# Weights prepared between the first graph's steps, on one core of a Trainium2 chip

## What is computed

```python
h = relu(layernorm(x));  x = x + L0(h, adj)     # 8-head attention over adj, then a sigmoid
h = relu(layernorm(x));  x = x + L1(h, adj)     # one symmetric attention, a gate
h = relu(layernorm(x));  x = x + L2(h, adj)     # 5 rounds of message passing with a GRU cell
h = relu(layernorm(x));  x = x + L3(h, adj)     # 1x1 and 17-tap convolutions, exp(-distance)
                                                # weights, a GRU cell
```

## Time and profile before

| | us |
|---|---|
| median of 3 runs | 2305.72 |
| lowest and highest run | 2302.09, 2308.01 |
| profiled execution, its own time | 2308.35 |
| span of the profiled execution | 2306.5 |

### The profile page before, as it was taken

The page is one execution under the profiler, slowest core; times in us unless marked ns, Lnnn a source line. Parts: engine busy times, 40 slices in busy tenths (PEclk is TensorE's granted clock), DMA queues, the critical chain, the costliest instruction groups (busy, mean ns, idle before and its releaser), DMA issues. The chain is left out here.

```text
span 2306.5 us, 36323 instructions
## 1 busy us (share of the span) xinstructions
PE 2122.3 (92%) x12626; PEld 1787.2 (77%) x12626; DVE 1666.9 (72%) x4784; ACT 1506.2 (65%) x2964; POOL 794.1 (34%) x888
## 2 busy tenths in 40 slices
PE   3889999998999999899998999999899999999966
PEld 3769788796978878787786978879697887868744
DVE  3668686877868787786867868687786868778643
ACT  1949485684948668395775939577494866849532
POOL 0333334342343434334243333333333343423311
PEclk7989999999999999999999999999999999999988
DMA  3010001010010101001010000101001010100100
GB/s 117 28 38 13 30 24 37 29 38 28 1 37 28 38 28 37 24 6 38 28 38 28 20 26 21 38 29 38 28 1 42 24 37 28 38 10 1 38 5 5
DMA packets 46791, 65.73 MB, mean 28 GB/s; under 512 B 3728, under 2 KB 21392, under 8 KB 46352
## 3 DMA queue, kind: packets, MB, share of 16 engines
q1 hardware_dynamic: 46608, 63.41, 8.4%
HBM read 59.21 MB, written 4.19 MB: 27 GB/s over the span
## 5 line engine op out<-in xcount | busy, mean ns | idle before, releaser
L573 PE MATMUL banks<-F,PT 128*128 128x128 f32 x4096 | 545.1, 276 | 3.5 <-ACT PT L834 2.8
L573 PEld LDWEIGHTS banks<-F,PT 128*128 128x128 f32 x4096 | 505.4, 192 | 27.6 <-issue 11.7
L1114 DVE COPY PT<-banks 128x512 f32<-128x512 f32 x256 | 176.1, 688 | 156.6 <-PE banks L567 156.1
L869 ACT ACTIVATE F<-banks,dcols 128x512 f32<-128x512 f32 x288 | 193.3, 682 | 27.1 <-PE banks L465 23.3
L431 POOL TENSOR_TENSOR HS<-HT,HS 128x512 fp32r<-128x512 f32 x64 | 83.3, 1301 | 366.7 <-ACT HS L898 366.7
L834 ACT ACTIVATE PT<-banks 128x512 f32<-128x512 f32 x256 | 150.4, 587 | 75.5 <-PE banks L567 75.2
L368 POOL TENSOR_TENSOR rstd<-var,mhalf 128x4 f32<-128x4 f32 x64 | 79.7, 1245 | 324.3 <-DVE var L1017 324.3
L398 POOL TENSOR_SCALAR tiles<-tiles,rden 128x512 f32<-128x512 f32 x192 | 131.9, 696 | 172.4 <-DVE rden L1104 172.2
L398 POOL TENSOR_SCALAR U<-U,rden 128x512 f32<-128x512 f32 x192 | 137.6, 729 | 134.7 <-DVE rden L1104 134.7
L461 PE MATMUL banks<-HS,WH 128*128 128x512 f32 (+1 forms) x368 | 165.2, 449 | 1.6 <-ACT HS L797 1.4
L398 POOL TENSOR_SCALAR adjT<-adjT,rden 128x512 f32<-128x512 f32 x128 | 93.8, 736 | 202.2 <-DVE rden L1104 202.2
(11 more groups left out here) (208 smaller groups left out, 5488.9 us busy)
## 6 DMA issues: line engine op xcount, KB each, us to landing
adjN<-in_adj_dram SPq DMA_DIRECT2D x32, 1024.0 KB, 5.2
adjT<-in_adjt_dram SPq DMA_DIRECT2D x16, 1024.0 KB, 5.4
xin<-in_x_dram SPq DMA_DIRECT2D x18, 256.0 KB, 2.8
out_dram<-X SPq DMA_DIRECT2D x16, 256.0 KB, 2.3
F<-in_c2w_dram SPq DMA_DIRECT2D x1, 1088.0 KB, 9.0
F<-in_wraw_dram SPq DMA_DIRECT2D x1, 1076.0 KB, 9.8
PT<-in_fcw_dram SPq DMA_DIRECT2D x1, 512.0 KB, 3.8
PT<-in_fpw_dram SPq DMA_DIRECT2D x1, 512.0 KB, 5.2
```

What stands on the lines that cost most here:

```text
L573: last = pe.matmul(B[s][:, 3, part(j)], PT[s][:, k, part(j)], G[s][:, k, h * DIM:(h + 1) * DIM], start=(h == 0 and j == 0 and k == 0), sto ...
L869: act.activation(F[s][:, tile, :], B[s][:, bank, :], func, bias=dcol(bias), scale=0.5)\
L1114: dve.tensor_copy(PT[s][:, j, :], pt_bank(s, j)).then_inc(S["pt_dve"], 1)
```

## The change

The setup block is taken apart into a strand called weights, which only graph 0 has, on TensorE (5 steps), ScalarE (5) and VectorE (9), and every weight array has its own semaphore. Loads are issued in the order cols, x of graph 0, the fc pair, adjacency of graph 0, raw weights, prew, c2, adjacency of graph 1, and, after waits for asym_banked and c2_low, x of graph 1. The staging places change: raw stays in F[1], prew goes to PT[1], c2 to adjT[1] and xin[1]. M and WI2 are no longer copied out of PSUM: ScalarE and VectorE split them from the banks.

```diff
+            load(cols[:, :], cols_d, cols_loaded)
+            inputs(0)
+            load(PT[0][:, 0:2, :].rearrange("p t n -> p (t n)"), fcw, fc_loaded)
+            load(PT[1][:, 0:2, :].rearrange("p t n -> p (t n)"), fpw, fc_loaded)
+            masks(0)
+            load(raw, wraw[:, 0:WALL - WRAW], raw_loaded)
...
+            masks(1)
+            sp.wait_ge(asym_banked, 1)
+            sp.wait_ge(c2_low, 1)
+            inputs(1)
...
-            pe.wait_ge(w_loaded, 7 * 16)
...
-            pe.wait_ge(w_split, 4)
+            def weights(g):
+                yield
+                if g > 0:
+                    return
...
+                pe.wait_ge(fc_loaded, 2 * 16)
+                pe.wait_ge(setup_dve, 2)
+                for h in range(HEADS):
+                    pe.matmul(B[1][:, 2, 2 * h:2 * h + 2], fcT[:, part(h)], cols[:, CI["qw"]:CI["qw"] + 2])
+                pe.matmul(B[1][:, 3, 0:HEADS], dcol("qkw").broadcast_to([P, P]), cols[:, 0:HEADS]).then_inc(vq_banked, 1)
+                yield
+                for h in range(HEADS):
+                    last = pe.matmul(B[1][:, h // 4, (h % 4) * DIM:(h % 4 + 1) * DIM], fcT[:, part(h)], fp[:, part(h)])
+                last.then_inc(m_banked, 1)
+                yield
+                pe.wait_ge(vq_ready, 1)
...
+                    .then_inc(m_banked, 1)
+                yield
+                pe.wait_ge(asym_ready, 1)
...
+                yield
+                pe.wait_ge(pre_loaded, 16)
+                pe.wait_ge(raw_ready, 1)
+                pe.wait_ge(m_low, 2)
...
+                last.then_inc(wi_banked, 1)
...
-            act.activation(WH[:, 0:WFIRST], stage[0], ACT.Copy).then_inc(w_split, 1)
-            act.activation(WH[:, WFIRST:WALL], stage[1][:, 0:WALL - WFIRST], ACT.Copy).then_inc(w_split, 1)
-            act.activation(VQH[:, :], VQ[:, :], ACT.Copy).then_inc(setup_act, 1)
-            act.wait_ge(setup_dve, 7)
+                act.wait_ge(vq_ready, 1)
+                act.activation(VQH[:, :], VQ[:, :], ACT.Copy).then_inc(vq_high, 1)
+                yield
+                act.wait_ge(m_banked, 1)
+                act.activation(WH[:, WFIRST:WRAW].rearrange("p (t n) -> p t n", t=2), B[1][:, 0:2, :], ACT.Copy).then_inc(m_high, 1)
+                yield
+                act.wait_ge(raw_ready, 1)
+                act.activation(WH[:, WRAW:WALL], raw, ACT.Copy).then_inc(raw_high, 1)
+                yield
+                act.wait_ge(wi_banked, 1)
...
+                act.activation(tiled(WH), adjT[1][:, :, :], ACT.Copy)
+                act.activation(WH[:, C2A:C2B], xin[1][:, 2, :], ACT.Copy).then_inc(c2_high, 1)
```

More of the change, by code:

```diff
@@ new lines @@
+    ("SP", "transfers"): (3515.678, 3562.397, 3562.397, 3575.622, 3634.067, 3711.988),
+    ("Pool", "inputs"): (3230.966, 3241.946, 3349.882),
+    ("Pool", "normalized"): (3291.779, 3291.779, 3291.779, 3291.779, 3291.779, 3291.779, 3293.808, 3298.303,
[31 rows of a table added]
+    ("Activation", "values"): (3320.761, 3330.097, 3334.275, 3344.175, 3345.848),
+    ("Activation", "weights"): (3235.044, 3313.964, 3344.300, 3360.600, 3389.275),
+    ("Activation", "softmax"): (3337.481, 3337.481, 3338.408, 3339.981, 3342.015, 3344.700, 3344.990, 3348.414,
[6 rows of a table added]
@@ L469, in W @@
                 return WH[:, a:a + n], WLO[:, a:a + n]
-            pe.wait_ge(w_loaded, 7 * 16)
-            fcT = PT[0][:, 0:2, :].rearrange("p t n -> p (t n)")
-            fp = PT[1][:, 0:2, :].rearrange("p t n -> p (t n)")
-            for h in range(HEADS):
-                pe.matmul(B[0][:, h // 4, (h % 4) * DIM:(h % 4 + 1) * DIM], fcT[:, part(h)], fp[:, part(h)])
-            for h in range(HEADS):
-                pe.matmul(B[0][:, 2, 2 * h:2 * h + 2], fcT[:, part(h)], cols[:, CI["qw"]:CI["qw"] + 2])
@@ L480, in _ @@
-            pe.wait_ge(setup_dve, 2)
-            pe.matmul(B[0][:, 3, 0:HEADS], dcol("qkw").broadcast_to([P, P]), cols[:, 0:HEADS])
-            for h in range(HEADS):
-                pe.matmul(B[1][:, 0, 0:DIM], cols[:, h:h + 1].broadcast_to([P, P]), fp[:, part(h)], start=(h == 0), stop=False)
-            pe.wait_ge(ident_ready, 2)
-            pe.matmul(B[1][:, 0, 0:DIM], col("fpb").broadcast_to([P, P]), ident[:, :], start=False, stop=True)
-            pre = PT[0][:, 2:4, :].rearrange("p t n -> p (t n)")
@@ L778, in taps, with weights @@
                 last.then_inc(S["c2_banked"], 1)
-            in_order("PE", values, keys, heads, layer1, layer2, layer3, taps)
+            in_order("PE", weights, values, keys, heads, layer1, layer2, layer3, taps)
         @block.scalar
         def _(act):
-            act.wait_ge(w_loaded, 7 * 16)
-            act.wait_ge(setup_dve, 3)
-            act.activation(WH[:, 0:WFIRST], stage[0], ACT.Copy).then_inc(w_split, 1)
-            act.activation(WH[:, WFIRST:WALL], stage[1][:, 0:WALL - WFIRST], ACT.Copy).then_inc(w_split, 1)
-            act.activation(VQH[:, :], VQ[:, :], ACT.Copy).then_inc(setup_act, 1)
-            act.wait_ge(setup_dve, 7)
+            def weights(g):
+                yield
+                if g > 0:
+                    return
+                act.wait_ge(vq_ready, 1)
[6 more added lines that the diff above has]
+                act.activation(WH[:, WRAW:WALL], raw, ACT.Copy).then_inc(raw_high, 1)
+                yield
+                act.wait_ge(wi_banked, 1)
+                for w, bank in zip(wi_parts(WH), wi_banks):
+                    last = act.activation(w, bank, ACT.Copy)
+                last.then_inc(wi_high, 1)
+                yield
+                act.wait_ge(c2_loaded, 2 * 16)
+                act.activation(tiled(WH), adjT[1][:, :, :], ACT.Copy)
+                act.activation(WH[:, C2A:C2B], xin[1][:, 2, :], ACT.Copy).then_inc(c2_high, 1)
             def h_high(g, turn):
@@ L944, in layer3 @@
                 cand_act(g, cell, "bih3n")
-            in_order("Activation", values, softmax, tile_copies, layer1, layer2, layer3)
+            in_order("Activation", weights, values, softmax, tile_copies, layer1, layer2, layer3)
         @block.vector
@@ L1318, in layer3 @@
                 add_residual(g, 3)
-            in_order("DVE", values, softmax, denominators, tile_copies, layer1, layer2, layer3)
+            in_order("DVE", weights, values, softmax, denominators, tile_copies, layer1, layer2, layer3)
 def kernel(**inputs):
```

192 lines of the change are left out of this document (123 added, 69 removed), and 102 rows, old and new, of the table TURN.

## The result

| | before | after |
|---|---|---|
| median, us | 2304.93 | 2184.37 |
| lowest and highest run, us | 2302.09 to 2308.01 | 2182.48 to 2186.99 |
| span of the profiled execution, us | 2306.5 | 2185.1 |

The ratio is 0.9477, with a 95% interval of 0.9461 to 0.9494.

The account below looks back on a forecast made before the run. TensorE, busy 92% of the span, was taken as the bound. From 2308.35 us, 25 for the front and 52.5 for graphs 1 to 15 (3.5 each) left 2230.9 profiled, median 2228 us; range 2208 to 2287.

Parts of the forecast that it names:

- The front: Stretch up to graph 0's tanh, 123.8 us before; the new setup was to save net 25 us, bounds 18 to 31.
- third weights step: TensorE's nine setup products ahead of graph 0's qk step, 18 matmul records, taken at 4.3 us.
- qk step: TensorE step after the third weights step in graph 0, taken at 2.8 us, giving QK at 23.3 us.
- the splits: ScalarE's raw, WI2 and c2 splits inside graph 0's softmax, 6248 columns, taken at full price, 5.5 us.
- Hole 1: TensorE's wait for layer 1's hN, slowed beside GpSimd's weights3 products; its removal was to save 3.9 us a graph.
- hole 2: TensorE's idle place between layer 3 of one graph and another's first steps; gain taken at zero, bounds -1 and +0.9.
- The dense stretch: Steps between the two holes, where TensorE does not idle; swaps there were to lose 0.4 us a graph, 2.5 at most.
- Theory C: Theory at the start of the experiments, not in the prediction: the order between the holes carries the rest of the gain.
- The first pitch: Spacing from graph 0's tanh to the next, 125.0 us before; forecast to gain 3.5 us like every later graph.
- Only the front: Rival: the order is neutral, 0 +/- 1.5 us a graph, only the setup gains; 2281 us, chance 0.32.
- weak front: Rival: the serial setup chain and softmax splits give back more, net 12 us at the front; 2241 us, chance 0.08.
- slower one: Rival: ScalarE runs dry between the holes, opening a third hole, 3.9 us a graph; 2339 us, chance 0.08.

Follow-up runs that it names:

- before_w3_wait: Kernel before, with GpSimd's four weights3 products waiting until the next graph's hN of layer 1 are done; 2240.9 us (0.9713).
- both waits: Kernel before, GpSimd's weights3 products waiting for the next graph's layer 1 hN, its second layer 1 product for layer 3's xc low part; 2228.9 us (0.9647).
- after_hole1_back_w3_wait: Changed kernel with hole 1's old order put back, and GpSimd's weights3 products waiting for the next graph's layer 1 hN; 2208.5 us (0.9574).
- after_hole2_back2: Changed kernel with the old order around hole 2 put back on TensorE, VectorE and ScalarE; 2195.3 us (0.9523).
- after_hole1_back: Changed kernel with the old order at hole 1 put back on TensorE, ScalarE and VectorE; 2224.8 us (0.9641).
- order_only: Kernel before, its setup kept, with the changed kernel's step order (START, TURN); 2216.6 us (0.9606).

## Why the prediction came out too high

**The front: right in kind, 5.9 us short.** First statistics were forecast near 5 us and came at 4.23; QK near 23 and came at 20.80, where it was at 56.69. Rows of ScalarE, VectorE and TensorE in the after kernel, timeline 0 to 26 us:

```profile
0.72 1.28 ACT L865 ACT_TABLE_LOAD   x1 [0.72 <-PEq L1490]
...
4.23 0.87 DVE L1115 BATCH_NORM_STATS2 bst<-xin 128x6 f32<-128x128 f32 x4
...
9.02 3.54 PE L531 MATMUL banks<-cols,PT 128*128 128x2 f32 x16 [9.02 <-DMA PT<-in_fpw_dram]
...
13.91 1.10 DVE L1129 TENSOR_SCALAR hN<-xin,mv,rstd 128x128 f32<-128x128 f32 x4
...
17.26 2.03 PE L540 MATMUL banks<-PT,cols 128*128 128x128 f32 x16
...
20.80 0.22 DVE L1168 TENSOR_TENSOR QK<-banks,CQ 128x64 f32<-128x64 f32 x1 [0.58 <-PE banks L512]
...
25.01 0.73 ACT L905 ACTIVATE U<-U,QN 128x513 f32<-128x513 f32 x1 [1.42 <-DVE U L1198]
```

Three terms were too dear. The table load (1.28 us) runs at 0.72, before any wait, not behind one. The third weights step takes 2.03 us for 16 matmuls, 0.13 each; I had taken 0.24 from L477. The same products had taken 0.24 in before too (L483), and in the after kernel the M products (L535), just ahead of the third step, still do:

```profile
21.72 3.76 PE L483 MATMUL banks<-PT,cols 128*128 128x128 f32 x16
```

```profile
12.86 3.76 PE L535 MATMUL banks<-PT 128*128 128x128 f32 x16
```

The windows give a granted clock of 1.00 for all three. But the first entry of the clock record is at 26.3 us in before and at 17.4 us in after, which is where the pace doubles; a clock of half speed until then would fit, and is not shown. And the qk step took 2.8 us in before because that stretch ran at half clock, which I could have read from the windows and did not (before, same columns as the windows above):

```profile
50.00:60.00 10.00, 6.92 (x25) 5.75 (x25) 4.37 (x11) 1.20 (x3) 1.33 (x1) 0.50 0.01 2
```

In after the same twelve small matmuls start every 0.11 us and take 1.3 us together. One term was too cheap: the fc pair landed at 9.02, not at 8.0. The first softmax step is 34.9 us earlier (I said 31); the splits cost 5.5 us as forecast; 34.9 - 5.5 = 29.4, and the front gained 30.9. The 1.5 us between, part of them in denser ScalarE windows, I leave unassigned, since they are within what fronts of one order differ by.

**Hole 1: the right mechanism, 0.7 us short.** I had 3.9 us a graph, 2.1 of idle time and 1.7 of clock, by moving aug and the taps. The clash alone is worth 4.57 (before_w3_wait). Idle time and clock at hole 1 are as forecast; what was left out is that a lower clock at hole 1 and one at hole 2 are not independent: the clock figure at hole 2 fell by 0.6 us too. Moving the chain of L1160 1.5 us earlier, the other half of my mechanism, need not have added to the pitch: with the old order at hole 1 and both waits it is 131.11, and less the 0.66 us of hole 2's order that is the changed kernel's 130.44. It was not tried by itself, and after_hole1_back_w3_wait (131.91), which has waits for R and the later products as well, does not settle it.

**"I take hole 2 at zero, bounds -1 and +0.9": failed.** The order there gives 0.66 us (after_hole2_back2), within the bounds. But the second clash, worth 0.85 us by the second wait, I had not seen at all. Its rows were in the trace of before. I had looked for GpSimd's neighbours only where TensorE waited longest, and took the 11.7 us for the cell's end as the chain's own length.

**The dense stretch: -0.4 us, failed.** The 81 us between the holes hold 0.2 us of idle time at clock 1.00, as the same windows show for before. Theory C has nothing left to carry. The sum 4.57 + 0.85 + 0.66 = 6.08 leaves nothing for it, against 6.09 measured. That the last term was measured from the other end, in the changed kernel, makes so close a match luck in part. And the split goes by the order in which things are taken away: starting from the changed kernel, hole 1 put back costs 2.6 us, not 4.57.

**The first pitch.** I gave it 3.5 us like the others; it gained 4.0. No other graph's products stand beside it, so it is not the clash; after_hole1_back has 123.57 there, so 2.6 of the 4.0 are hole 1's order. The other 1.4 were not tried one by one.

**The rivals.** Only the front (0.32) fell with order_only, and the weak front (0.08) with the front's 30.9 us. The slower one (a third hole in the dense stretch) has no trace in any kernel. Against my range: its low end, 2208 us, lies 24 us above the result. It held no room for a term that I had not listed, and the second clash alone is 12 us; nor for hole 1 to be worth more than my 3.9 us, and that is 9 more.

In terms of the forecast: of the 43.6 us, 5.9 are the front, 14 x 0.67 = 9 hole 1's clash, 14 x 0.85 = 12 the second clash, 14 x 0.66 = 9 hole 2's order, 14 x 0.4 = 6 the loss that did not come, and 2 the first pitch and the tail.

## What to carry to other kernels

Before costing an order of steps, list each instruction group whose mean is longer than its like elsewhere in the same kernel, on VectorE and GpSimd above all, and look what the other engine runs at that moment: two such pairs held 5.4 of the 6.1 us a graph here, and one wait on the less urgent engine took out each of them. Undo a change of order on every engine that reads the moved step, or the experiment measures a stall of its own. Before calling a clash intermittent, look at its durations graph by graph; the clock behind it can be what changes. And read the granted clock of the stretch before taking a duration from it into a sum.

## What the runs showed of the hardware

Idle time of TensorE can cost about double where the clock falls behind it: at hole 1 of before, 2.1 us of idle time had 1.7 us of clock with it, and taking the clash away gave 4.57 us of pitch, with what came back at hole 2. The clock's cost at a hole is not a constant of the order. With the same steps, the clock figure of hole 2 was 0, 1.7 or 3.4 us from graph to graph in the changed kernel, and the pitch 129.6 to 131.4 us. In after_hole1_back the same 1.8 us of idle time at hole 1 was followed by half clock in four of 11 graphs and by full clock in seven, with pitches of 134.4 to 134.6 us against 131.7 to 133.3; the clash was on in all of them (4.4 us for four hN in one of each kind). So a clash must be judged by durations taken graph by graph, and a pitch by the granted clock beside it.
